# A routed feed-forward layer on one core: five row buffers, gathers issued in pairs, and expert results handed over 128 columns at a time

## What is computed

```python
h = _layernorm(x) * (1 + cb) + sb
route_prob = softmax(h @ Ws + bs).T                 # 8 experts x 4096 tokens
route_vals, routes = top_k(route_prob, 512)         # each expert takes its 512 best tokens
xin = h[routes]                                     # gather
y = gelu(xin @ W1[e] + b1[e]) @ W2[e] + b2[e]       # 128 -> 512 -> 128
y = y * route_vals[..., None]
final = zeros.at[routes].add(y)                     # scatter with addition
x = x + gb * final
```

## Time and profile before

| | |
|---|---|
| median of 3 runs (range) | 352.97 us (352.78 to 354.15) |
| the profiled execution: time, span | 356.2 us, 354.5 us |
| busy: PE, DVE, ACT, POOL | 69%, 59%, 46%, 50% of the span |
| mean granted TensorE clock | 0.863 of 2.4 GHz |
| gathers | 32 issues on POOL, first start 234.6 us, last start 309.4 us |
| scatters | 32 issues on POOL, first start 259.8 us, last start 345.4 us |

### The profile page before, as it was taken

How to read it: one execution, slowest core, us unless ns; L and a number is a source line. 1 busy time by engine, 2 the same in 40 slices (tenths; PEclk the granted TensorE clock), 3 DMA queues, 4 the chain that set the end, 5 groups by cost and what they waited for, 6 DMA issues and landing times.

```text
span 354.5 us, 8066 instructions
## 1 busy us (share of the span) xinstructions
PE 246.0 (69%) x3056; PEld 174.3 (49%) x3056; DVE 210.8 (59%) x675; ACT 162.3 (46%) x223; POOL 177.3 (50%) x221
## 2 busy tenths in 40 slices
PE   1689989999999999999743411226899966976000
PEld 1346657676676767777522300113566663764000
DVE  4164898989898999979784588694042302212100
ACT  5267758786867858686500365102133403202000
POOL 5507347373646637350615000047557887777661
PEclk9999999999999999999995565555999988789555
DMA  7607201010101001010113999924313433442321
GB/s 216 172 3 281 81 17 47 17 47 9 40 15 30 30 15 44 18 48 18 32 30 58 89 99 275 251 41 111 96 16 76 59 56 76 65 49 24 30 22 15
DMA packets 30542, 24.06 MB, mean 68 GB/s; under 512 B 6368, under 2 KB 27184, under 8 KB 30128
## 3 DMA queue, kind: packets, MB, share of 16 engines
q0 software_dynamic: 6848, 9.06, 18.0%
q1 hardware_dynamic: 23664, 14.59, 13.8%
HBM read 15.11 MB, written 8.54 MB: 67 GB/s over the span
## 4 chain that ended last, share of the span: by engine, by line
DVE 32%; POOL 24%; issue 14%; PE 13%; DMA 6%; ACT 5%; another core or an unknown queue 2%; DVEq 1%; SPq 0%; POOLq 0%; ACTq 0%
POOL out_y L570 13%; POOL rstd L481 3%; POOL area L560 3%; ACT area L703 3%; DVE y_s L785 3%; DMA modb<-mod_rows 3%; DMA out_y<-o_sb,idx 3%; DVE low L1058 2%; DVE y_n L790 2%; PE ps L1145 2%; DVE xn L825 2%; DVE area L750 2%; DVE wgt L760 2%; POOL vare L479 2%
## 5 line engine op out<-in xcount | busy, mean ns | idle before, releaser
L634 ACT ACTIVATE wgt<-ps 128x1024 f32<-128x1024 f32 x64 | 62.3, 1028 | 37.0 <-PE ps L1145 37.0
L570 POOL DMA_INDIRECT out_y<-o_sb,idx x32 | 50.7, 1583 | 21.2 <-issue 8.5
L560 POOL DMA_INDIRECT area<-token_rows,idx x32 | 31.0, 969 | 52.0 <-DVE idx L1071 42.5
L1145 PEld LDWEIGHTS ps<-area 32*128 32x128 f32 x1024 | 42.1, 184 | 24.8 <-ACT wgt L644 13.9
L1145 PE MATMUL ps<-area 32*128 32x64 f32 (+3 forms) x1024 | 50.2, 321 | 2.9 <-ACT wgt L634 1.2
L714 ACT ACTIVATE area<-ps,b_sb 128x512 f32<-128x512 f32 x32 | 21.4, 687 | 53.8 <-PE ps L1347 53.5
L1175 PE MATMUL ps<-wgt,v_bd 128*32 128x259 f32 (+3 forms) x1024 | 42.0, 304 | 3.8 <-DVE y_t L776 3.1
L1357 PE MATMUL ps<-modb,area 128*128 128x128 f32 x256 | 35.3, 304 | 2.5 <-ACT area L714 2.5
L1357 PEld LDWEIGHTS ps<-modb,area 128*128 128x128 f32 x256 | 34.3, 219 | 4.3 <-ACT area L714 4.3
L1175 PEld LDWEIGHTS ps<-wgt,v_bd 128*32 128x32 f32 x1024 | 29.0, 109 | 14.9 <-DVE y_t L776 4.4
L1347 PE MATMUL ps<-area,xall 128*128 128x512 f32 x64 | 31.5, 626 | 2.4 <-issue 1.3
(11 more groups left out here) (181 smaller groups left out, 441.9 us busy)
## 6 DMA issues: line engine op xcount, KB each, us to landing
modb<-mod_rows SPq DMA_DIRECT2D x3, 1024.0 KB, 7.5
out_y<-x SPq DMA_DIRECT2D x16, 128.0 KB, 1.8
token_rows<-h SPq DMA_DIRECT2D x16, 128.0 KB, 1.9
token_rows<-gb_mod POOLq DMA_DIRECT2D x1, 2048.0 KB, 28.1
xall<-in_w SPq DMA_DIRECT2D x1, 2048.0 KB, 28.7
modb<-in_w SPq DMA_DIRECT2D x8, 256.0 KB, 6.4
xall<-in_x SPq DMA_DIRECT2D x2, 768.0 KB, 8.0
xall<-in_x SPq DMA_DIRECT2D x2, 256.0 KB, 4.4
```

Of the source, the lines that this page charges most:

```text
L560: eng.indirect_dma_start(out=xg[e % 4][:, j, :], out_offset=None, in_=rows[:, :], in_offset=bass.IndirectOffsetOnAxis(ap=idx[:, e, j:j + 1 ...
L570: eng.indirect_dma_start(out=out[:, :], out_offset=bass.IndirectOffsetOnAxis(ap=idx[:, e, j:j + 1].bitcast(u32), axis=0), in_=o_sb[e % 2][ ...
L634: k = nc.scalar.activation(wgt[bb][:, 2 * half:2 * half + 2, :, 0:256], ps[:, 2 * half:2 * half + 2, :].rearrange("p c (a q) -> p c a q", ...
L1145: return mm(ps[:, cc, col:col + SEQ - key * BK], k_bd[par][qd][r, 4 * bb + key, :, :].rearrange("p a k -> p (a k)"), q_sb[par][qd][r, t0 + ...
```

## The change

There are five row buffers instead of four (`NXG = 5`; the fifth lies in memory that the threshold search used) and three result buffers instead of two (`NOB = 3`). POOL issues the gathers of experts 0 to 4 in a row, then alternates: a scatter of four issues, then two issues of the next gather, down to the last pair (second half of expert 7) between the scatters of experts 5 and 6; the scatters of 6 and 7 follow each other. `s_o` and `s_op` are raised for each column group of 128 (4 per expert), TensorE waits for VectorE's read of the group two before, the groups alternate between PSUM banks 4 and 5, and VectorE does the bias in four operations of 128 columns, each followed by its multiplication. Each of the four issues of a scatter waits for its own group. For experts 5 and 6 the second layer and the result come ahead of the transposition and copy of the next expert's rows.

```diff
--- before.py
+++ after.py
@@ setup @@
+    NXG = 5
+    NOB = 3
...
-              for n in range(4)]
-        at = HALF + 4 * CT * ROW
+              for n in range(NXG - 1)]
+        xg.append(area_f[:, 0:CT * ROW].rearrange("p (j r) -> p j r", j=CT))
+        at = HALF + (NXG - 1) * CT * ROW
...
-        o_sb = [sb(f"o_sb{n}", [P, CT, D], fp32) for n in range(2)]
+        o_sb = [sb(f"o_sb{n}", [P, CT, D], fp32) for n in range(NOB)]
...
-        s_xg = [sem(f"gathered{n}") for n in range(4)]
+        s_xg = [sem(f"gathered{n}") for n in range(NXG)]
@@ -551,25 +554,26 @@
             eng.dma_start(rows[:, D:2 * D].rearrange("(b n) d -> b n d", b=NB),
                           gb_mod[:, :].unsqueeze(1).broadcast_to([NB, SEQ, D])).then_inc(s_gbrow, 16)
 
-            def gather(e):
-
-                eng.wait_ge(s_idx, e + 1)
-                if e >= 4:
-                    eng.wait_ge(s_o, e - 3)
-                for j in range(CT):
-                    eng.indirect_dma_start(out=xg[e % 4][:, j, :], out_offset=None, in_=rows[:, :],
+            def gather(e, j0=0, j1=CT):
+
+                if j0 == 0:
+                    eng.wait_ge(s_idx, e + 1)
+                    if e >= NXG:
+                        eng.wait_ge(s_o, CT * (e - NXG + 1))
+                for j in range(j0, j1):
+                    eng.indirect_dma_start(out=xg[e % NXG][:, j, :], out_offset=None, in_=rows[:, :],
                                            in_offset=bass.IndirectOffsetOnAxis(ap=idx[:, e, j:j + 1].bitcast(u32), axis=0))\
-                       .then_inc(s_xg[e % 4], 16)
+                       .then_inc(s_xg[e % NXG], 16)
 
             def scatter(e):
 
-                eng.wait_ge(s_o, e + 1)
                 if e:
                     eng.wait_ge(s_sc, 16 * CT * e)
                 for j in range(CT):
+                    eng.wait_ge(s_o, CT * e + j + 1)
                     eng.indirect_dma_start(out=out[:, :],
                                            out_offset=bass.IndirectOffsetOnAxis(ap=idx[:, e, j:j + 1].bitcast(u32), axis=0),
-                                           in_=o_sb[e % 2][:, j, :], in_offset=None, compute_op=ALU.add)\
+                                           in_=o_sb[e % NOB][:, j, :], in_offset=None, compute_op=ALU.add)\
                        .then_inc(s_sc, 16)
 
             for bb in range(2):
@@ -577,12 +581,22 @@
                 eng.wait_ge(s_h2o[bb], 16 * UNITS + 16)
             eng.wait_ge(s_gbrow, 16)
             eng.wait_ge(s_pro, 16)
-            for e in range(3):
+            for e in range(NXG):
                 gather(e)
-            for e in range(NE):
-                if e + 3 < NE:
-                    gather(e + 3)
-                scatter(e)
+            scatter(0)
+            gather(5, 0, 2)
+            scatter(1)
+            gather(5, 2, 4)
+            scatter(2)
+            gather(6, 0, 2)
+            scatter(3)
+            gather(6, 2, 4)
+            scatter(4)
+            gather(7, 0, 2)
+            scatter(5)
+            gather(7, 2, 4)
+            scatter(6)
+            scatter(7)
             eng.wait_ge(s_sc, 16 * CT * NE)
 
 
@@ -1079,23 +1093,25 @@
             eng.wait_ge(s_bias, 32)
             x_copy(0)
             for e in range(NE):
-                if e + 1 < NE:
+                if e + 1 < NXG + 1:
                     x_copy(e + 1)
 
-                eng.wait_ge(s_op, e + 1)
-                if e:
-                    eng.wait_ge(s_o, e)
-                nc.vector.tensor_tensor(o_b[:, :, :], ps[:, 4 + e % 2, :].rearrange("p (j d) -> p j d", j=CT),
-                                        b2_sb[:, e:e + 1, :].broadcast_to([P, CT, D]), ALU.add).then_inc(s_ob, 1)
-                eng.wait_ge(s_ob, e + 1)
-                if e >= 2:
-                    eng.wait_ge(s_sc, 16 * CT * (e - 1))
-                g = xg[e % 4]
+                if e >= NOB:
+                    eng.wait_ge(s_sc, 16 * CT * (e - NOB + 1))
+                g = xg[e % NXG]
                 for j in range(CT):
-                    k = nc.vector.scalar_tensor_tensor(o_sb[e % 2][:, j, :], o_b[:, j, :],
-                                                       g[:, j, 2 * D + e:2 * D + e + 1], g[:, j, D:2 * D],
-                                                       ALU.mult, ALU.mult)
-                k.then_inc(s_o, 1)
+                    n = CT * e + j
+                    eng.wait_ge(s_op, n + 1)
+                    if e:
+                        eng.wait_ge(s_o, n - CT + 1)
+                    nc.vector.tensor_tensor(o_b[:, j, :], ps[:, 4 + j % 2, j * P:(j + 1) * P], b2_sb[:, e, :], ALU.add)\
+                        .then_inc(s_ob, 1)
+                    eng.wait_ge(s_ob, n + 1)
+                    nc.vector.scalar_tensor_tensor(o_sb[e % NOB][:, j, :], o_b[:, j, :],
+                                                   g[:, j, 2 * D + e:2 * D + e + 1], g[:, j, D:2 * D],
+                                                   ALU.mult, ALU.mult).then_inc(s_o, 1)
+                if NXG <= e < NE - 1:
+                    x_copy(e + 1)
 
 
         @block.tensor
@@ -1327,13 +1343,13 @@
 
             def to_x_t(e):
 
-                eng.wait_ge(s_xg[e % 4], 16 * CT * (e // 4 + 1))
+                eng.wait_ge(s_xg[e % NXG], 16 * CT * (e // NXG + 1))
                 if e == 1:
                     eng.wait_ge(s_idx, 6)
                 if e >= 2:
                     eng.wait_ge(s_xt, e - 1)
                 for j in range(CT):
-                    k = tr(ps[:, 6 + e % 2, j * P:(j + 1) * P], xg[e % 4][:, j, 0:D], ident[:, :])
+                    k = tr(ps[:, 6 + e % 2, j * P:(j + 1) * P], xg[e % NXG][:, j, 0:D], ident[:, :])
                 k.then_inc(s_xtp, 1)
 
             to_x_t(0)
@@ -1345,18 +1361,20 @@
                     else:
                         eng.wait_ge(s_idx, k + 2)
                     mm(ps[:, k, :], w1_sb[:, e, k * P:(k + 1) * P], x_t[e % 2], start=True, stop=True).then_inc(s_h1, 1)
-                if e + 1 < NE:
+                if e + 1 < NXG + 1:
                     to_x_t(e + 1)
                 eng.wait_ge(s_g, FC * e + FC)
                 if e < 2:
                     eng.wait_ge(s_idx, 7 + e)
-                if e >= 2:
-                    eng.wait_ge(s_ob, e - 1)
                 for j in range(CT):
+                    if CT * e + j >= 2:
+                        eng.wait_ge(s_ob, CT * e + j - 1)
                     for k in range(FC):
-                        last = mm(ps[:, 4 + e % 2, j * P:(j + 1) * P], g_sb[:, k, j * P:(j + 1) * P], w2_sb[:, e, k, :],
+                        last = mm(ps[:, 4 + j % 2, j * P:(j + 1) * P], g_sb[:, k, j * P:(j + 1) * P], w2_sb[:, e, k, :],
                                   start=(k == 0), stop=(k == FC - 1))
-                last.then_inc(s_op, 1)
+                    last.then_inc(s_op, 1)
+                if NXG <= e < NE - 1:
+                    to_x_t(e + 1)
 
 
 def kernel(L0_attn_hidden_states, L0_attn_Wq, L0_attn_Wk, L0_attn_Wv, L0_attn_Wo, L0_ffn_Ws, L0_ffn_bs, L0_ffn_W1,
```

## The result

| | before | after |
|---|---|---|
| median of 5 runs | 353.42 us (352.78 to 354.15) | 350.55 us (349.88 to 350.90) |
| ratio | | 0.9914, interval 0.9892 to 0.9936 |
| the profiled execution: time, span | 356.2, 354.5 | 350.9, 349.2 |
| predicted | | 346.1, range 343.3 to 349.6 |

The changed kernel is faster by 0.9%, 2.9 us. 6.8 were forecast, and the time lies 0.95 us above the range. Against the medians that the kernel before had beside the later runs, 352.62 to 353.05, the gain is 2.1 to 2.5 us.

The account below looks back on a forecast made before the run. Bound: POOL's issues and scatter landings from 234 us on. POOL's stream without other waits ends at 345.3 (gain 9.2); plus 2.4 for expert 7 gives 347.7 against 354.5; 6.8 off the 352.97 median gives 346.1, range 343.3 to 349.6.

Parts of the forecast that it names:

- Part 1: Ahead of the first scatter: four more gathers (5.0 us) cost nothing, hidden by POOL's idle 5.25 us; scatter starts at 259.8.
- rival 2: First scatter 3.8 us late if VectorE's unexplained wait at expert 0 moves with the gathers; 349.9 us; chance 9%.
- Part 2: POOL's stream from 259.8 on: six rounds take 61.1 us, landing waits hidden except ahead of expert 7; gain 9.2 us.
- Part 3: POOL's scatter issues: 24 added waits cost 0 beyond the usual 0.30 us gap.
- Part 4: Experts 1 to 6 keep up with POOL's 10.2 us round; the new order for experts 5 and 6 costs nothing.
- Part 5: Ahead of the last scatter: expert 7's first column comes 2.4 us late; 0.5 at full clock, 5.05 at half.
- Rival 1: At the last scatter: expert 7 in time, clock stays up or column chain is shorter; 343.8 us; chance 22%.
- Rival 3: At the 32 scatter issues: VectorE's separated multiplications block POOL, up to 0.35 us each, +10.0, 356.1 us; chance 7%.
- Rival 4: TensorE stays at half clock between experts, work per expert grows towards 15 us; about 358 us; chance 2%.

Follow-up runs that it names:

- rows_first: Changed kernel with the next expert's transposition and copy ahead of the second layer for experts 5 and 6 too, as before; 352.86 us, ratio 1.0002.
- whole_gathers: Changed kernel with the gathers of experts 5, 6 and 7 in groups of four behind scatters 0, 1 and 2 instead of pairs; 351.91 us, ratio 0.9978.
- pair_earlier: Changed kernel with the last pair of gathers (second half of expert 7) one scatter earlier; 348.36 us, ratio 0.9876.
- before_again: The kernel before, unchanged, run and profiled a second time; 352.75 us, ratio 1.0002.
- before_third: The kernel before, unchanged, profiled a third time in a single execution; 354.02 us.
- warm_expert7: Changed kernel with nine 512-column matmuls, results unread, in TensorE's pause ahead of expert 7's transposition; 347.76 us, ratio 0.9866.
- no_columns: Changed kernel with results handed over per expert again (one 512-column bias addition, one signal); 354.93 us, ratio 1.0060.

## Why the prediction was wrong

**Part 1 was the failed step.** It counted "POOL's idle 5.25 us" ahead of the first scatter as the cover of four gathers. The idle time was right for that execution and is not the kernel's: two further profiles of it show 1.4 and 2.4 us, because the 4 us in which VectorE didn't start were in the first profile alone. Without the stall the four early gathers take 5.0 us of POOL's time and only 1.4 or 2.4 of idle time stand against them. 3.8 or 2.9 us of the forecast gain did not exist. The signs were on the page: the profiled execution took 356.2 us, 3.2 above the median of the runs and 2.0 above their highest, and rival 2 named the unexplained wait. It asked only whether the wait would move with the gathers, not whether it was there in other executions. The sum was taken against the disturbed profile and then subtracted from the undisturbed median, and that step lost the 3 to 4 us. Subtracted from the time of the profiled execution itself it would have given 356.2 - 6.8 = 349.4, 1.1 under the measured 350.55. What caused the stall no run shows; it was in one of three profiles of the kernel before, and in none of the ten of the changed kernel and its variants, where VectorE starts on expert 0's result as soon as TensorE has it. ScalarE and TensorE were held up in the same 4 us. Both VectorE and ScalarE wait there for signals of TensorE, whose own stream has gaps, so the cause is rather to be sought at TensorE or beyond it than in VectorE's work; that is argued and not shown.

**Part 2 was right to 0.1 us.** From the first scatter to scatter 6: predicted 61.1, measured 321.48 - 260.46 = 61.0. A pair costs 2.58 to 2.66. No wait for landing stands ahead of scatters 1 to 6. The first scatter came at 260.46 instead of 259.8 because the first gather started at 235.28 instead of 234.62, held by the store of the probabilities, as in both new profiles of before; the change doesn't touch that store. From the last scatter's start to the end: 14.7 predicted, 349.2 - 334.41 = 14.8.

**Part 3 was right:** the added waits that were satisfied show the gap of 0.30 and nothing more.

**Part 4 was right:** no wait ahead of scatters 1 to 6, and rows_first shows that the new order isn't free of effect: it is what keeps expert 6 in time. "Costs nothing" was true and said too little: undone, it costs the whole gain.

**Part 5 had the mechanism and was 0.9 short.** Scatter 7 could start at 327.14 + 4.03 = 331.2 and started at 334.41: 3.2 late, 2.35 predicted. From transposition to second layer it took 331.65 - 323.05 = 8.6 instead of 8.3, 0.3 more: the first layer took 5.92 where expert 0's row had 5.44, and the steps around it were 0.2 shorter. The first column came 0.1 later than taken. The largest part is POOL's start after the multiplication, 0.83 (333.58 to 334.41) where the first scatter of before had given 0.3: a term taken from one row, and 0.5 too small. The bias addition of 128 columns took 0.29, 0.35 was taken. The Trainium skill's page "VectorE: DVE Perf Modes", section "The TRN2 errata — SBUF-src ops pay a fixed extra latency per instruction", gives an addition of N float32 columns as (N + 151) / 0.96 ns, measured there for 512 and 2048 columns; an estimate by it for 128 is 0.29 us, and this trace agrees.

Two smaller slips of part 5 change nothing in the outcome. The 4.03 for landing belongs to the order of waits of before; with the changed kernel's order landing alone gave 3.5 to 3.7 (whole_gathers, pair_earlier), so the last expert was 3.5 to 3.8 late against what POOL could have done. And the lateness at the half level adds up to 2.35 + 2.8 = 5.15, not 5.05.

**The sum with the right terms:** 6.8 less 3.8 less 0.9 is 2.1 against before_again (measured from the first gather's start to the end of the span, 115.8 against 113.9: 1.9), and 6.8 less 2.9 less 0.9 is 3.0 against before_third (117.0 against 113.9: 3.1). The medians differ by 2.9, and by 2.1 to 2.5 against the later medians of the kernel before.

**The rivals.** Rival 1 (expert 7 in time) is what warm_expert7 makes: its lateness is 331.25 - (326.72 + 4.03) = 0.5, the value given for the full clock level. The changed kernel itself had 8 us of idle TensorE and the half clock, as the prediction held against this rival. Rival 2 fell, with its premise: the first scatter waits for nothing. Rival 3 fell: the median scatter issue is 1.568 us against 1.564 of before. The issue at 276.45 has a multiplication of expert 3 inside it and took 1.56 (kernel after, timeline):

```profile
276.45 1.56 POOL L574 DMA_INDIRECT out_y<-o_sb,idx  x1 [0.30 <-DVE o_sb L1110]
...
276.81 0.35 DVE L1110 SCALAR_TENSOR_TENSOR o_sb<-area 128x128 f32<-128x128 f32 x1
```

So the rule of the Trainium skill's page "SBUF — State Buffer", section "Who interferes with whom", that a VectorE instruction with two SBUF inputs contends with a GpSimd instruction that reads SBUF, does not hold up this issue. The same section infers that writing descriptors needs the shared write interface, which such a VectorE instruction doesn't take; the prediction left that out, and the 1.56 us agree with it, though no run here shows the reason. Rival 4 fell for experts 1 to 5: the second layers of experts 0 to 3 start 8.05 us apart, expert 4's 8.6 later, each first layer of experts 1 to 5 takes 3.60, and the clock is 1.00 from 250 to 294 us. Only behind the pauses of 8 us, at experts 6 and 7, is it at its half level again. On the clock the page "TensorE: Matmul & The Clock Gate" of the Trainium skill, section "HAM oscillation — how this bites in real kernels", says that matmuls which come in bursts between waits for DMAs start each burst at the lower clock. This kernel agrees at experts 0, 6 and 7, whose first layers start at a granted clock of 0.50 and take 5.41, 5.82 and 5.92 us, and the filled pause shows the reverse.

**Where the expected gain went.** Of the 9.2 us without any new wait, 3 to 4 were an event of one execution, and 3.2 came back as the wait for the last expert. What is left is the idle time at the first scatter and two of three waits for landing, less the lateness of expert 7. Each idle time of the rows holds the ordinary gap of 0.30, which stays: without it these are 1.1 to 2.1, twice 2.2, and 3.2, which gives 2.3 to 3.3, and 1.9 to 3.1 were measured. (The prediction's 12.6 us for all four waits hold four such gaps too; its sum doesn't use that figure.) The edits hang together: without columns or without the new order the gain is gone, since expert 7's rows come late only through the pairs, and both shorten what follows from that. Only the early place of expert 4's gathers can be given up.

## What to carry to other kernels

Before a wait is counted as a gain, see whether it is there in a second profile, above all when the profiled execution is slower than every plain run: subtract from the time of the execution in which the wait stands, not from the median. When gathers are spread to hide other waits, look at the last one: what depends on it starts late and on a cold engine, and it may be cheaper to leave one wait bare (pair_earlier) or to keep TensorE at work through the pause (warm_expert7) than to hide everything.

## What the runs showed of the hardware

TensorE's granted clock was 0.50 behind a pause of 8 us, and the next first layer took 5.92 us against 3.70; nine matmuls whose result nobody reads, put into the pause, kept the clock at 1.00 and made the kernel faster by 2.8 us (medians) or 1.7 (ratios).

A wait for landed scatters that blocks POOL directly in front of an indirect DMA costs more than the same wait one instruction earlier: 4.09 and 4.08 us against 3.48 and 3.70 from issue to issue, with nothing else exchanged. For a wait for VectorE's column it is only suggested: 0.83 against 0.47 from VectorE's end. The 0.83 is steady where a scatter stands ahead: after, warm_expert7, no_columns (337.79 to 338.62) and rows_first have it at the last scatter. The first scatter of the kernel before, behind gathers, started 0.28 after its release (256.36 to 256.64 in before_again) although its wait was the one directly in front. So the order isn't the whole of it; whether it is that gathers and not a scatter stand ahead was not tried.
